# One kernel of deformable convolution and routed experts: the stages of its interleaved bodies are given new places

## What is computed

```python
def conv(inputs):                                  # inputs = layernorm(x)
    x_proj = inputs @ w_in + b_in
    x1 = gelu(layernorm(depthwise3x3(inputs)) * gamma + beta)
    offset = x1 @ w_off + b_off                    # 8 groups x 9 taps x 2
    mask = softmax(x1 @ w_mask + b_mask, over the 9 taps)
    px, py = pixel + tap + offset                  # sampling positions
    samp = bilinear_gather(pad(x_proj), px, py)    # 4 corners, zero outside
    return sum_over_taps(samp * mask) @ w_out + b_out

def ffn(t):                                        # t = layernorm(x)
    logits = t @ Wr + br;  probs = softmax(logits);  top 2 of 8 experts
    y_e = gelu((norm(t) * ln_g[e] + ln_b[e]) @ W1[e] + b1[e]) @ W2[e] + b2[e]
    return sum over the top two of weight_e * y_e

x = x + conv(layernorm(x))
x = x + ffn(layernorm(x))
```

## Time and profile before

| | us |
|---|---|
| median of 3 runs | 309.98 |
| lowest, highest | 307.35, 310.00 |
| the profiled execution | 309.92 |
| its span, first to last instruction | 308.1 |
| mean granted TensorE clock | 0.972 |
| busy: PE, DVE, ACT, POOL | 269.5, 238.4, 190.3, 120.6 |

### The profile page before, as it was taken

The page is one execution under the profiler, slowest core; times in us unless marked ns, Lnnn a source line. Parts: engine busy times, 40 slices in busy tenths (PEclk is TensorE's granted clock), DMA queues, the critical chain, the costliest instruction groups (busy, mean ns, idle before and its releaser), DMA issues.

```text
span 308.1 us, 8247 instructions
## 1 busy us (share of the span) xinstructions
PE 269.5 (87%) x3312; PEld 178.5 (58%) x3312; DVE 238.4 (77%) x680; ACT 190.3 (62%) x351; POOL 120.6 (39%) x123
## 2 busy tenths in 40 slices
PE   6975999774897998899799999988978999989795
PEld 2552467542565766354477765535757788677462
DVE  6999868999977589995889589998757446189455
ACT  3786446573753397788365678775545685746363
POOL 6230132310750431405096605050575373648530
PEclk9998999999897899999999999997999999999999
DMA  5920000000000000000000000000000000000000
GB/s 149 291 54 0 2 3 3 3 0 0 2 2 0 2 4 3 2 0 2 0 2 20 2 3 0 2 0 2 3 17 2 2 3 2 9 2 2 10 2 17
DMA packets 7187, 4.83 MB, mean 16 GB/s; under 512 B 5089, under 2 KB 6830, under 8 KB 7086
## 3 DMA queue, kind: packets, MB, share of 16 engines
q1 hardware_dynamic: 7150, 4.31, 5.7%
HBM read 2.04 MB, written 0.52 MB: 8 GB/s over the span
## 4 chain that ended last, share of the span: by engine, by line
PE 43%; DVE 39%; POOL 10%; issue 4%; ACT 2%; DMA 1%; DVEq 0%; POOLq 0%; ACTq 0%
DVE prod L891 6%; DVE samp L906 4%; PE ga_ps L1579 4%; PE z_ps L1547 3%; PE z_ps L1549 3%; PE ga_ps L1581 3%; PE m_ps L1681 3%; PE ga_ps L1580 3%; PE z_ps L1561 3%; POOL prod L566 2%; PE m_ps L1648 2%; PE m_ps L1693 2%; PE m_ps L1664 2%; PE m_ps L1650 2%; PE m_ps L1471 2%
## 5 line engine op out<-in xcount | busy, mean ns | idle before, releaser
L1306 ACT ACTIVATE wk<-z_ps 128x512 int32<-128x512 f32 x108 | 64.6, 598 | 56.4 <-PE z_ps L1549 55.9
L1579 PE MATMUL ga_ps<-v_all,wk 128*128 128x80 f16 x576 | 79.3, 204 | 11.4 <-DVE prod L891 11.1
L891 DVE TENSOR_TENSOR prod<-ga_ps,wx 128x480 f32<-128x480 f32 x96 | 61.6, 650 | 27.6 <-PE ga_ps L1581 27.3
L566 POOL TENSOR_TENSOR prod<-prod 128x960 f32<-128x960 f32 (+1 forms) x20 | 36.5, 1825 | 113.5 <-DVE prod L891 113.5
L1579 PEld LDWEIGHTS ga_ps<-v_all,wk 128*128 128x128 f16 x576 | 57.7, 101 | 38.4 <-issue 17.3
L1580 PE MATMUL ga_ps<-v_all,wk 128*128 128x80 f16 x576 | 79.2, 204 | 0.0
L1581 PE MATMUL ga_ps<-v_all,wk 128*128 128x80 f16 x576 | 79.1, 204 | 0.0
L1580 PEld LDWEIGHTS ga_ps<-v_all,wk 128*128 128x128 f16 x576 | 58.2, 101 | 7.9 <-issue 1.1
L1581 PEld LDWEIGHTS ga_ps<-v_all,wk 128*128 128x128 f16 x576 | 58.4, 101 | 0.0
L1547 PE MATMUL z_ps<-tab,sel_hi 128*128 128x512 f16 x108 | 42.6, 394 | 0.5 <-ACT tab L1298 0.5
L1549 PE MATMUL z_ps<-tab,sel_lo 128*128 128x512 f16 x108 | 42.4, 393 | 0.0
(11 more groups left out here) (279 smaller groups left out, 577.0 us busy)
## 6 DMA issues: line engine op xcount, KB each, us to landing
v_all<-still SPq DMA_DIRECT2D x1, 1440.0 KB, 10.7
h_all<-in_W SPq DMA_DIRECT2D x1, 512.0 KB
w_s<-in_W SPq DMA_DIRECT2D x1, 512.0 KB
x_tok<-in_x SPq DMA_DIRECT2D x1, 384.0 KB, 6.7
out_dram<-x_tok SPq DMA_DIRECT2D x6, 64.0 KB, 1.7
w_high<-w_high SPq DMA_DIRECT2D x1, 256.0 KB, 3.0
const<-in_table SPq DMA_DIRECT2D x1, 218.0 KB, 2.7
vec<-in_vectors SPq DMA_DIRECT2D x1, 132.5 KB
```

The source lines that it names most:

```text
L566: then(pool.tensor_tensor(p[:, 0:3, :], p[:, 0:3, :], p[:, 3:6, :], ALU.add))
L891: dve.tensor_tensor(prod[q % 2][:].rearrange("p k n -> p (k n)")[:, f * PB * NV:(f + 1) * PB * NV] .rearrange("p (n c l) -> p n c l", n=PB ...
L1306: act.activation(wk[n % WR][:], z_ps[use % 2][:], ACT.Relu, scale=HIGH_UNIT * FINE / Z_UNIT).then_inc(s_wk, 1)
L1579: pe.matmul(to, w_h, high, start=True, stop=False)
```

## The change

All tables of places get new numbers: those of bodies 0, 1 and 2 on all four engines, and of body 3 the back's, the half chunk's, `zeros`, `lane_sums` and POOL's. Entries that no body uses stay. No stage, instruction, buffer or wait is added or removed; what changes is the order in which each engine issues its stages. The diff shows the tables that the steps below need; those of ScalarE and POOL in body 0 and of all but TensorE in body 2 are left out ("..."). Three patterns run through it: in bodies 1 and 2 the convolution, the offsets and all that follows them stand 6 to 12 places later; the experts of the chunk before, which were spread from 11.5 to 30, stand in the second half with four `expert_out` from 28 on; in body 3 the experts of chunk 2 stand from 36 to 71.5 instead of 17.5 to 48, and the first half of chunk 3's back from 69 on instead of 50.

```diff
-PE_FIRST = {"input_t": 4, "convolve": [7, 8.5, 8.5, 9.5], "project": 6.5, "image_t": [10, 11.5], "conv_t": 14.5, "offsets":
-            15.5, "table": [24.5, 27], "samples_t": 24.5, "project_out": 8.5, "experts_t": 17.5, "router": 27, "expert_in":
-            [22, 35.5, 35.5, 35.5, 35.5, 35.5, 35.5, 35.5, 35.5, 35.5, 35.5, 35.5, 35.5, 35.5, 35.5, 35.5], "expert_out":
-            [17, 17.5, 20.5, 21, 21, 22.5, 25, 30], "outputs_t": [29.5, 30], "b2": 0, "bias_product": [0, 0, 1, 1, 3, 4, 4.5,
-            5.5], "zeros": [19, 22, 18.5]}
...
-DVE_FIRST = {"input_stats": 13.5, "input_norm": 31, "input_low": 2.5, "conv_stats": 10.5, "project_low": 6, "conv_norm":
-             11.5, "image_out": 11.5, "positions": [14.5, 15, 15], "rows": [16.5, 19, 21.5, 22], "edges": 23, "hats": 25.5,
-             "tap_weights": [23, 27.5], "lane_sum": [9, 9, 18.5, 20.5, 31.5, 33.5, 3, 5], "residual": 10, "inner_norm": 32.5,
-             "zn_low": 17, "route": [18, 23, 25.5], "expert_weights": 26, "b2": 0, "bias_rows": 5, "router_parts": 31,
-             "w1_low": [1.5, 9.5, 13.5, 20.5], "outputs_in": [30.5, 26.5], "second_stats_": 25, "second_norm": 0.5}
...
-PE_SECOND = {"input_t": 0, "convolve": [5, 5.5, 6, 10], "project": 4, "image_t": [11, 12], "conv_t": 14, "offsets": 15.5,
-             "table": [35.5, 35.5], "samples_t": 3, "project_out": 4, "experts_t": 7.5, "router": 11.5, "expert_in": [11.5,
-             13, 13.5, 13.5, 16, 17, 18.5, 18.5, 19, 19, 22.5, 23, 24.5, 25, 27, 28], "expert_out": [18, 22, 26.5, 30],
-             "outputs_t": [34.5, 35.5], "b2": 17.5}
-PE_THIRD = {"input_t": 1, "convolve": [5.5, 6, 7.5, 8], "project": 5, "image_t": [9.5, 12.5], "conv_t": 14, "offsets": 15,
-            "table": [31.5, 35.5], "samples_t": 3, "project_out": 4, "experts_t": 8, "router": 11, "expert_in": [12, 13,
-            13.5, 14, 16.5, 16.5, 18.5, 19, 20.5, 21, 22.5, 23, 24.5, 25, 27, 28], "expert_out": [18, 22, 26.5, 31.5],
-            "outputs_t": [33.5, 34], "b2": 9.5}
-ACT_SECOND = {"pad_image": 0.5, "project_high": 4.5, "image_out": 11.5, "conv_gelu": 14.5, "tap_exp": 16.5, "distances":
-              [20.5, 21.5, 22, 22, 26.5], "samples_out": 3.5, "zn_out": 10.5, "router_exp": 17.5, "hidden": [12.5, 12.5, 15,
-              15.5, 17.5, 17.5, 18.5, 18.5, 21.5, 22, 23, 23.5, 26, 26.5, 27.5, 28.5], "outputs_out": [19.5, 25.5, 29.5,
-              33.5]}
...
-DVE_SECOND = {"input_stats": 12.5, "input_norm": 13.5, "input_low": 1.5, "conv_stats": 9, "project_low": 6, "conv_norm":
-              10.5, "image_out": 11, "positions": [14, 16, 14], "rows": [16, 19.5, 20, 27.5], "edges": 22, "hats": 29,
-              "tap_weights": [29, 34.5], "lane_sum": [13.5, 14.5, 19.5, 22, 28, 28, 1, 1], "residual": 4, "inner_norm": 4.5,
-              "zn_low": 8.5, "route": [10.5, 16, 17.5], "expert_weights": 23, "b2": 8.5, "bias_rows": 21, "router_parts":
-              14.5, "w1_low": [0.5, 7, 12, 13.5], "outputs_in": [34, 35]}
...
+PE_FIRST = {"input_t": 6.5, "convolve": [10, 10.5, 10.5, 10.5], "project": 10, "image_t": [13, 15.5], "conv_t": 17,
+            "offsets": 18, "table": [34, 34], "samples_t": 24.5, "project_out": 8.5, "experts_t": 17.5, "router": 27,
+            "expert_in": [22, 35.5, 35.5, 35.5, 35.5, 35.5, 35.5, 35.5, 35.5, 35.5, 35.5, 35.5, 35.5, 35.5, 35.5, 35.5],
+            "expert_out": [17, 17.5, 20.5, 21, 21, 22.5, 25, 30], "outputs_t": [29.5, 30], "b2": 3.5, "bias_product": [0, 16,
+            17.5, 22, 24.5, 27.5, 27.5, 27.5], "zeros": [32, 34, 31]}
...
+DVE_FIRST = {"input_stats": 10.5, "input_norm": 16, "input_low": 6.5, "conv_stats": 9.5, "project_low": 8.5, "conv_norm": 13,
+             "image_out": 14.5, "positions": [17, 20, 23.5], "rows": [21, 21.5, 27.5, 31], "edges": 17.5, "hats": 32.5,
+             "tap_weights": [31.5, 35.5], "lane_sum": [16, 16, 23.5, 24.5, 31, 35, 3, 5], "residual": 10, "inner_norm": 32.5,
+             "zn_low": 17, "route": [18, 23, 25.5], "expert_weights": 26, "b2": 2.5, "bias_rows": 27, "router_parts": 8,
+             "w1_low": [3.5, 4.5, 8, 8], "outputs_in": [30.5, 26.5], "second_stats_": 25, "second_norm": 3.5}
...
+PE_SECOND = {"input_t": 2.5, "convolve": [13.5, 15.5, 7, 7.5], "project": 12, "image_t": [17, 18.5], "conv_t": 22.5,
+             "offsets": 27, "table": [33.5, 35.5], "samples_t": 9, "project_out": 10, "experts_t": 15.5, "router": 17.5,
+             "expert_in": [19, 19, 19.5, 20, 22, 23, 24.5, 25, 28.5, 30, 31, 31, 31.5, 31.5, 32.5, 33], "expert_out": [29,
+             31, 33, 33.5], "outputs_t": [35, 35.5], "b2": 17.5}
+PE_THIRD = {"input_t": 3, "convolve": [18, 17.5, 12.5, 18], "project": 8, "image_t": [15, 22], "conv_t": 25, "offsets": 26,
+            "table": [33.5, 35.5], "samples_t": 6.5, "project_out": 10, "experts_t": 16, "router": 19.5, "expert_in": [20.5,
+            21.5, 22, 25, 25.5, 26.5, 28.5, 29, 30, 30.5, 31, 31.5, 31.5, 32.5, 33, 33], "expert_out": [28, 31, 33, 33.5],
+            "outputs_t": [35, 35.5], "b2": 9.5}
+ACT_SECOND = {"pad_image": 4, "project_high": 12, "image_out": 17, "conv_gelu": 22, "tap_exp": 28, "distances": [31, 31, 31,
+              31.5, 33], "samples_out": 8.5, "zn_out": 15, "router_exp": 27.5, "hidden": [18, 18.5, 20, 21.5, 23, 23.5, 24.5,
+              25.5, 29, 29.5, 30, 30, 31, 31, 31.5, 32], "outputs_out": [30, 32.5, 33.5, 33.5]}
...
+DVE_SECOND = {"input_stats": 8, "input_norm": 22.5, "input_low": 2.5, "conv_stats": 18.5, "project_low": 12.5, "conv_norm":
+              20, "image_out": 16.5, "positions": [25.5, 27, 25.5], "rows": [27.5, 29.5, 30, 30.5], "edges": 27, "hats":
+              30.5, "tap_weights": [28, 34], "lane_sum": [20, 14.5, 21.5, 24, 34, 35.5, 5, 6], "residual": 8.5, "inner_norm":
+              12.5, "zn_low": 14.5, "route": [16, 20, 22.5], "expert_weights": 28, "b2": 8.5, "bias_rows": 21,
+              "router_parts": 14.5, "w1_low": [0.5, 7, 12, 13.5], "outputs_in": [35, 35]}
...
-POOL_SECOND = {"tap_tree": [8.5, 16, 16.5, 16.5], "combine": [17, 29], "conv_rstd": 14, "inner_rstd": 7, "input_rstd": 15}
...
+POOL_SECOND = {"tap_tree": [0, 10, 23, 28.5], "combine": [29, 35.5], "conv_rstd": 19, "inner_rstd": 3.5, "input_rstd": 3.5}
...
 PE_LAST = {"input_t": 0, "convolve": [0, 0, 0, 0], "project": 0, "image_t": [16.5, 35], "conv_t": 42.5, "offsets": 19,
-           "table": [45.5, 47.5], "samples_t": 4.5, "project_out": 4.5, "experts_t": 11, "router": 15, "expert_in": [17.5,
-           19.5, 20, 22, 24.5, 27.5, 29, 29, 31.5, 34, 35.5, 37.5, 40.5, 41.5, 43.5, 45.5], "expert_out": [22.5, 26, 32, 32,
-           42.5, 44.5, 46.5, 48], "outputs_t": [34.5, 55.5], "b2": 0.5, "half_samples_t": 50, "half_project_out": 50.5,
-           "half_experts_t": 57.5, "half_router": 60.5, "zeros": [3.5, 6]}
+           "table": [45.5, 47.5], "samples_t": 14, "project_out": 16.5, "experts_t": 32, "router": 42, "expert_in": [36, 45,
+           47.5, 49, 54, 55.5, 56.5, 60.5, 60.5, 61, 61, 61.5, 63, 64.5, 65, 65], "expert_out": [50.5, 60.5, 61, 64.5, 69,
+           70.5, 71.5, 71.5], "outputs_t": [66, 71.5], "b2": 0.5, "half_samples_t": 69, "half_project_out": 69,
+           "half_experts_t": 71.5, "half_router": 71.5, "zeros": [18, 32]}
 ACT_LAST = {"pad_image": 0, "project_high": 61, "image_out": 10.5, "conv_gelu": 23, "tap_exp": 0, "distances": [18.5, 37.5,
-            38.5, 42.5, 57.5], "samples_out": 4, "zn_out": 11, "hidden": [18.5, 19.5, 20, 21.5, 26.5, 27, 29, 30.5, 31, 33,
-            36.5, 38.5, 41, 44, 45.5, 46], "outputs_out": [32, 48], "half_samples_out": 48.5, "half_zn_out": 57}
+            38.5, 42.5, 57.5], "samples_out": 15.5, "zn_out": 32.5, "hidden": [44.5, 44.5, 48, 49, 54.5, 55.5, 57, 58.5,
+            59.5, 59.5, 61, 61, 63.5, 63.5, 65, 65.5], "outputs_out": [63.5, 71], "half_samples_out": 66, "half_zn_out": 71}
 DVE_LAST = {"input_stats": 70.5, "input_norm": 42.5, "input_low": 0, "conv_stats": 29.5, "project_low": 0, "conv_norm": 26,
-            "tap_weights": [56.5, 71.5], "lane_sum": [0, 0, 2.5, 5, 7.5, 18.5, 0, 0.5], "residual": 0.5, "inner_norm": 4,
-            "zn_low": 10.5, "route": [16, 19, 33], "expert_weights": 36, "b2": 40, "bias_rows": 40.5, "router_parts": 18.5,
-            "w1_low": [10.5, 18, 24.5, 32.5], "outputs_in": [37, 54], "half_residual": 46, "half_inner_norm": 47.5,
-            "half_zn_low": 55.5, "half_route": [57.5, 58, 67], "half_expert_weights": 69.5, "lane_sums": [13.5, 26.5, 31,
-            45.5, 54.5, 64.5, 71]}
-POOL_LAST = {"tap_tree": [2, 10.5, 15, 33.5, 38, 47, 63, 63.5], "combine": [42.5, 68], "conv_rstd": 62, "inner_rstd": 1.5,
-             "input_rstd": 6, "half_inner_rstd": 44.5, "router_exp": 21, "half_router_exp": 57}
+            "tap_weights": [56.5, 71.5], "lane_sum": [0, 0, 2.5, 5, 7.5, 18.5, 2, 2.5], "residual": 15, "inner_norm": 24,
+            "zn_low": 32, "route": [40.5, 54.5, 58], "expert_weights": 62.5, "b2": 40, "bias_rows": 40.5, "router_parts":
```

(5 more changed lines are left out.)

## The result

The changed kernel takes 280.83 us (median of 4 runs, 280.4 to 282.66) against 309.99 us before: a ratio of 0.909 (95% interval 0.903 to 0.915), 9% faster. The forecast was 305.3 us with a range of 299 to 315. Two later sets of runs gave 0.914 (0.908 to 0.920) and 0.913 (0.907 to 0.918), where the kernel before had medians of 308.0 and 307.9 us.

The account below looks back on a forecast made before the run. TensorE and VectorE were nearly full; time with neither full was winnable. Start 31.3, bodies 56.1, 65.0, 65.9, 60.0 and tail 25.7 gave 304.0 us, 305.8 with 1.8 around, 305.3 after half a microsecond off; range 299 to 315.

Parts of the forecast that it names:

- stretch sums: Each body cut into stretches, the largest engine sum of each added up: 53.5, 60.4, 61.0 us in bodies 0 to 2.
- The residues stay as they are: Bodies 0 to 2: the 2.6, 4.6 and 4.9 us unexplained by the sums were kept unchanged in the new layout.
- as many hits as before: VectorE instructions delayed by POOL trees, about 2 us each, were taken as equally many in the new layout.
- third rival: Bodies 0 to 2: two more collisions with POOL trees in each, run slower at 313 to 317 us; chance 0.15.
- The stretch of four places as a wall: Bodies 0 to 2: engines overlap inside a four-place stretch, not beyond; its largest engine sum sets its time.
- The 4.1 us wait: Body 0: TensorE's 4.1 us wait for the last feature row before `features_t` was to go.
- the lump on VectorE: Body 0, before: 10.2 us of VectorE's work in one stretch against TensorE's 3.9, right ahead of `table`.
- The lane sums' 2.1 us: Body 1: TensorE's 2.1 us wait for lane sums before `samples_t` was to go, with those stages moved later.
- the 4.0 us for fills: Body 1: TensorE's 4.0 us of waits for fills, listed in the earlier trace, to shrink only at best.
- better fit: Dense ends overlap wholly and residues shrink by listed fill waits of 2.8 and 4.0 us: about 299 us; chance 0.12.
- The tail held: Tail: to stay at 25.7 us, with both POOL `combine` ending 2 us before the last `inner_rstd`'s input.

Follow-up runs that it names:

- the moved tables: Kernel before with only `table` in body 0 moved from 24.5 and 27 to 29 and 31 on TensorE: 307.38 us, 0.996.
- at place 10: Changed kernel with four extra VectorE memsets at place 10 of bodies 1 and 2, 1.8 us a body: 284.08 us, 0.923 to the kernel before.

## Why the prediction was wrong

**What bounds the kernel.** Right in kind: bodies 1 and 2 came out as long as TensorE is busy in them, 57.90 of 57.90 us and 57.40 of 57.50. The stretch sums gave 60.4 and 61.0, before any residue.

**"The residues stay as they are": the step that failed most.** The old bodies were 2.6, 4.6 and 4.9 us longer than the sums of their largest parts. I named latencies, the low clock and collisions as what they hold, and then carried all three over whole, as if no order could change them. They belonged to the old order and in part to that one execution: the trees cost 2.6, 2.8 and 1.9 us at equal clocks, and stretches at the low clock 3.1 us in body 1 and 1.5 in body 2. Without the 12.1 us of residue the forecast's span of 303.5 us would have been 291.4; 279.3 was measured, so the sums themselves were another 12 us too long. The forecast showed a collision row by row, and then took "as many hits as before", and its third rival went the wrong way: more hits in the dense end. It did not follow for each tree which VectorE instructions come while it runs. In the new order, in the tree that was followed, these are lane sums, fills and positions. Body 2's waits were not listed at all; there the 2.1 us for one fill, which a tree brought on, stood in the trace of the kernel before.

**The stretch of four places as a wall.** For body 2 it gave 2.5 us more and 6.7 less came, 5.2 of them at equal clocks. Two runs speak against the wall. Late in a body, where TensorE has experts to do, 1.0 and 0.8 of 1.8 us added on VectorE came through in the body itself, and 0.7 more showed up in body 3. And the sums treat a lean stretch as harmless because VectorE's sum there is smaller than TensorE's, while 1.2 and 2.0 of 1.8 us came through at place 10; the old front lay in such places. Moving front and experts late together, which I read as a danger, did no harm in any of the new bodies. That it is the cover, TensorE's long stages beside VectorE's, is argued: the back moved alone cost 13.9 us, but by three things at once, and the front moved alone wasn't run.

**Body 0.** The 4.1 us wait went, for which I gave the right cause (the lump on VectorE, not the place of `table`), as the moved tables showed. The gain of 8.5 us instead of 3.2 is more than the 4.1 and 2.8 us of waits of the earlier trace rows together; a wait of 1.7 us for VectorE's part of the image (`v_all`) went too, which the forecast doesn't list. The trees' 2.6 us partly stand behind these and can't be added to them. The 2.1 us of the DMA train were missed: I counted the moved `bias_rows` on VectorE and not the sixteen issues behind it.

**Body 1.** The lane sums' 2.1 us went as forecast, and so did the 4.0 us for fills, which the forecast kept but for its "better fit". Behind body 1's first unit the list of waits of bodies 1 and 2 is empty.

**Body 3 and tail.** Forecast 0.1 longer, measured 3.1 shorter. By the list of waits: before `half_router` 1.2 (forecast 1.75), before the last `outputs_t` 1.0 (1.3), samples 0.5 (0.75). The rest of the difference was in the lean part, where I laid nothing out: the old body had 4.8 us without a busy TensorE, the new one 3.5, and waits for fills of 2.2 us became 0.9. The tail held: 25.2 us, with POOL's exponential and both `combine` ahead of the last `inner_rstd` (260.73 us in the chain), as forecast.

**Range and chances.** 280.8 us lies far below 299. The better fit was worked out as full overlap and only took off listed waits; the low clock and the trees were nowhere in it. A lower figure was at hand: the start, TensorE's busy times in the old bodies and the tail, 31.3 + 49.5 + 61.9 + 59.8 + 55.1 + 25.7 = 283.3 us of span. Even that isn't a bound, since the busy times hold the low clock; 279.3 us was measured.

**Open.** At equal clocks 5.9, 5.2 and 3.3 us of the gains of bodies 0, 1 and 2 are more than the trees cost there. They went together with TensorE's waits for features, fills, image and lane sums, but how they part between stages too early for their inputs and lumps without cover isn't shown; removing the trees also moves the lane sums. Why the low clock stands behind the same waits in one execution and not in another isn't known, nor what its first stretch costs in body 0.

## What to carry to other kernels

When an interleaved order is laid anew, bound the gain by the fullest engine's own sum, and take nothing of the gap between that and the old time as given: ask of each part of it whether the order made it. Check VectorE's work between two buffers, not over a stretch, against what TensorE has to do in that time, and try the long stages of both beside each other. For each long POOL instruction look which VectorE instructions run beside it, and for each moved stage at the DMAs that hang on it.

## What was not expected of the hardware

The same unchanged code was run at a granted clock of 0.86 over 25 us in one profile and of 1.00 in another, 3.1 us apart in a body, and another body at 0.97 and 1.00, 1.4 apart: one profiled execution can hold a loss that the kernel need not have. A VectorE instruction of 0.30 us took 2.33 beside a POOL addition of 2.22 us, while fills and positions, which read PSUM, kept their 0.65 and 0.37 us beside one of 2.21, and so did lane sums, which read SBUF. "GPSIMD Engine Reference" of the Trainium skill (section Specifications) puts that contention on the shared SBUF interfaces, for Vector instructions in a two-port mode or with two SBUF inputs. The rows agree as far as they go: `shape`, with two inputs, took 1.12 us for 0.45; `xa` has one, and no trace shows its mode. Leaving the additions out was worth 7.3 us in three bodies. Sixteen DMA issues of 0.5 KB took 10.6 us of one queue.
